# A rank search inside an attention loop: masks counted by VectorE instead of GpSimd and TensorE, and two context weights multiplied once

## What is computed

```
x = layernorm(x + attention0(x))        # 16 heads of width 8, plus a "splat" flow of 64 points
x = layernorm(x + cross0(x, context))   # the value path of the context: (c Wv^T + bv) Wo^T + bo
```

## Time and profile before

| | |
|---|---|
| median of 3 runs | 2092.27 us (2090.64 to 2105.77) |
| the profiled execution | 2103.81 us, span 2102.1 us |
| first loop, first to last score maximum | 46.13 to 493.35 us of the span |
| busy over the span: PE, PEld, DVE, ACT, POOL | 86%, 66%, 66%, 59%, 50% |
| granted TensorE clock, mean over the span | 0.90 of full |
| masks on GpSimd (line 946) | 128 x, 1563 ns each, 198.0 us busy |

### The profile page before, as it was taken

The page is one execution under the profiler, slowest core; times in us unless marked ns, Lnnn a source line. Parts: engine busy times, 40 slices in busy tenths (PEclk is TensorE's granted clock), DMA queues, the critical chain, the costliest instruction groups (busy, mean ns, idle before and its releaser), DMA issues. The chain is left out here.

```text
span 2102.1 us, 44035 instructions
## 1 busy us (share of the span) xinstructions
PE 1798.3 (86%) x15604; PEld 1391.5 (66%) x15604; DVE 1387.6 (66%) x4638; ACT 1247.6 (59%) x3006; POOL 1042.5 (50%) x1594
## 2 busy tenths in 40 slices
PE   3999999999588999999999999999849999569940
PEld 2666666666476778777777777877635666459940
DVE  3767777774467777777777887787646887341127
ACT  1465555654377777787777777776513777334412
POOL 0546655563335555565555565566421332246455
PEclk9789998996699999999999999999967999669975
DMA  4000000000200000000000000000000000054422
GB/s 56 9 6 14 14 15 14 8 11 8 85 1 1 5 1 7 7 7 7 7 4 4 7 7 7 4 5 5 7 24 9 22 27 19 17 117 79 66 59 81
DMA packets 70240, 44.81 MB, mean 21 GB/s; under 512 B 26560, under 2 KB 62538, under 8 KB 69834
## 3 DMA queue, kind: packets, MB, share of 16 engines
q1 hardware_dynamic: 55384, 29.79, 5.2%
q0 software_dynamic: 4608, 9.45, 3.1%
q10 hardware_dynamic: 10034, 2.77, 0.7%
HBM read 27.31 MB, written 14.16 MB: 20 GB/s over the span
## 5 line engine op out<-in xcount | busy, mean ns | idle before, releaser
L2105 POOL TENSOR_SCALAR probs<-probs,rsums 128x128 f32<-128x128 f32 (+1 forms) x512 | 208.3, 425 | 325.7 <-DVE rsums L2004 325.6
L946 POOL TENSOR_SCALAR at_least<-magnitudes,candidates 128x512 bf16<-128x512 f32 x128 | 198.0, 1563 | 210.6 <-DVE candidates L842 210.6
L1988 DVE CUSTOM_DVE_ANT_0 probs<-dist,pq,nmin 128x128 f32<-128x128 f32 (+1 forms) x512 | 181.2, 409 | 128.5 <-PE pq L1480 127.8
L1735 ACT ACTIVATE probs<-probs,low 128x130 f32<-128x130 f32 (+1 forms) x512 | 227.6, 460 | 3.7 <-DVE low L1988 3.6
L913 DVE TENSOR_REDUCE negmax<-ps_scores 128x4 f32<-128x1024 f32 x128 | 156.5, 1223 | 103.7 <-PE ps_scores L573 102.4
L731 ACT ACTIVATE pT<-ps_scoresT 128x1024 f32<-128x1024 f32 x128 | 131.2, 1025 | 77.4 <-PE ps_scoresT L582 70.4
L1998 DVE COPY pT<-pq 128x384 f32<-128x384 f32 x256 | 130.2, 550 | 2.7 <-PE pq L1495 2.7
L1657 ACT ACTIVATE qn<-pq 128x512 f32<-128x512 f32 x128 | 77.0, 602 | 79.9 <-PE pq L1352 78.4
L1480 PE MATMUL pq<-k1T,q1T 64*128 64x128 f32 (+1 forms) x1024 | 119.6, 352 | 1.5 <-DVE low L1988 1.4
L3083 POOL DMA_INDIRECT m_x<-token_rows,m_idx_put x80 | 75.8, 947 | 80.0 <-DVE m_idx_put L3013 32.8
L3035 DVE COPY m_y<-pm 128x256 f32<-128x256 f32 x40 | 17.0, 425 | 140.3 <-PE pm L2921 140.3
(11 more groups left out here) (527 smaller groups left out, 5545.4 us busy)
## 6 DMA issues: line engine op xcount, KB each, us to landing
expert_answers<-m_y SPq DMA_DIRECT2D x40, 128.0 KB, 2.1
m_w<-in_L_ffn_moe_w_dram SPq DMA_DIRECT2D x16, 256.0 KB, 6.0
x<-in_x_dram SPq DMA_DIRECT2D x16, 128.0 KB, 2.1
x_mid<-x SPq DMA_DIRECT2D x16, 128.0 KB, 1.8
y<-x_mid SPq DMA_DIRECT2D x16, 128.0 KB, 2.2
x_mid<-y SPq DMA_DIRECT2D x16, 128.0 KB, 1.8
cx<-x_mid SPq DMA_DIRECT2D x8, 256.0 KB, 3.1
token_rows<-c_hn SPq DMA_DIRECT2D x8, 256.0 KB, 2.0
```

What stands on the lines that cost most here:

```text
L946: pool.tensor_scalar(at_least[:, a, :], mags[:, 512 * (a // 2):512 * (a // 2) + 512], cf[:, a:a + 1], None, ALU.is_ge).then_inc(mask_ready ...
L1735: ins = act.activation(probs[:, a, keys_nulls(i, w)], probs[:, a, keys_nulls(i, w)], ACT.Exp, bias=low[:, a, i:i + 1], scale=-1.0, accum_o ...
L1988: ins = dve.tensor_tensor_reduce(probs[:, a + t, keys(i, w)], dist[:, (1 - t) * P:N], ps[:, t * P:t * P + w], slopes[h], nmin[u][:, t, h:h ...
L2105: ins = pool.tensor_scalar(probs[:, a + t, keys(i, w)], probs[:, a + t, keys(i, w)], rsums[:, a + t, i:i + 1], 1.0, ALU.mult, ALU.mult)
```

## The change

VectorE now makes the masks itself, with the form of compare that also adds up its result along the row (`row_counts`). A single product with ones sums the eight row counts over the partitions, and `decide` compares that product in PSUM with the ranks. Four mask instructions of a decision are spread over two steps; `decide` moves one step earlier. GpSimd keeps only its part of the normalisations in this loop.

For the context, Wv and Wo are multiplied once (`fold_cross`, at step 16 of the loop), with bv Wo^T added to the bias row; `three_parts` moves there. `cross_values` is gone, and `cross_out` multiplies the stored context `cT` (six buffers in place of two) with the folded weight.

```diff
@@ stages
-            (8, "max_rows"), (24, "mixed"), (27, "project_out"), (31, "cross_out"), (22, "normalise"),
-            (5, "decide0"), (9, "decide1"), (1, "candidates0"), (5, "candidates1"),
+            (8, "max_rows"), (24, "mixed"), (27, "project_out"), (16, "fold_cross"), (31, "cross_out"), (22, "normalise"),
+            (4, "decide0"), (8, "decide1"), (1, "masks00"), (2, "masks01"), (5, "masks10"), (6, "masks11"),
...
-            (-10, "project_x"), (-1, "vg"), (1, "cross_values"), (3, "influence_tm"), (6, "encode"),
-            (4, "count0"), (8, "count1"), (10, "transform"), (11, "read_transform"), (12, "decode"), (14, "flow"),
+            (-10, "project_x"), (-1, "vg"), (3, "influence_tm"), (6, "encode"),
+            (3, "count0"), (7, "count1"), (10, "transform"), (11, "read_transform"), (12, "decode"), (14, "flow"),
@@ TensorE
-            def cross_values(u):
-                pe.wait_ge(*cT_ready.at(u + 1))
-                ps = ring.open(pe, "vx", u, held=0.7)
-                pe.matmul(ps[:, 0:S_CTX + 1], wv_x[:], cT[u][:], start=True, stop=True).then_inc(ring.filled("vx", u), 1)
+            def fold_cross(u):
+                if u:
+                    return
+                pe.wait_ge(bias3_ready, 1)
+                ps = ring.open(pe, "w_x", held=0.9)
+                pe.matmul(ps[:, 0:D], wv_raw[:], wo_x[:], start=True, stop=True)
+                pe.matmul(ps[0:3, D:2 * D], bv_x[:], wo_x[:], start=True, stop=True).then_inc(ring.filled("w_x"), 1)
...
-                pe.wait_ge(*mask_ready.at(4 * (n + 1)))
                 pe.wait_ge(*small_ready.at(n + 1))
-                ps = ring.open(pe, "count", n, held=1.7)
-                for a in range(4):
-                    for q in range(8):
-                        pe.matmul(ps[:, a * 64:(a + 1) * 64], ones_bf[:], at_least[:, a, q * 64:(q + 1) * 64],
-                                  start=(q == 0), stop=(q == 7))
-                pe.matmul(ps[:, 256:272], ones_sq[:], at_least_small[:].rearrange("p a n -> p (a n)"),
-                          start=True, stop=True).then_inc(ring.filled("count", n), 1)
+                ps = ring.open(pe, "count", n, held=1.3)
+                pe.matmul(ps[:, 0:8], ones_sq[:], row_counts[:], start=True, stop=True).then_inc(ring.filled("count", n), 1)
...
-                    pe.matmul(ps[:, t * D:(t + 1) * D], vx[u][:, t * P:(t + 1) * P], wo_x[:], start=True, stop=False)
+                    pe.matmul(ps[:, t * D:(t + 1) * D], cT[u][:, t * S_CTX:t * S_CTX + P], w_x[:], start=True, stop=False)
@@ VectorE
-            three_parts(dve, setup, bo_x3, bo_x, bo_work, pick)
+            dve.tensor_copy(bv_x[:, 1:3], bv_x[:, 0:1].broadcast_to([P, 2])).then_inc(bias3_ready, 1)
...
+                link(dve.tensor_tensor(bo_x[:], bo_x[:], ps[0:3, D:2 * D], ALU.add))
+                dve.sem_inc(ring.read("w_x"), 1)
+                three_parts(dve, link, bo_x3, bo_x, bo_work, pick)
+                dve.sem_inc(parts_ready, 1)
...
+                for a in (2 * part, 2 * part + 1):
+                    chain.add(dve.tensor_scalar(at_least[:, a, :], mags[:, 512 * part:512 * part + 512], cf[:, a:a + 1], None,
+                                                ALU.is_ge, ALU.add, accum_out=row_counts[:, a:a + 1]))
+                if part:
+                    link(dve.tensor_tensor(at_least_small[:], mags_small[:], cf[:, 4:8].unsqueeze(2).broadcast_to([P, 4, 4]),
+                                           ALU.is_ge))
+                    dve.tensor_reduce(row_counts[:, 4:8], at_least_small[:], AX.X, ALU.add).then_inc(small_ready.sem, 1)
 
             def decide(n):
                 ps = ring.wait(dve, "count", n)
-                link(dve.tensor_reduce(counts[:, 0:4], ps[:, 0:256].rearrange("p (a n) -> p a n", a=4), AX.X, ALU.add))
-                dve.tensor_reduce(counts[:, 4:8], ps[:, 256:272].rearrange("p (a n) -> p a n", a=4), AX.X, ALU.add)\
-                    .then_inc(ring.read("count", n), 1)
+                dve.tensor_tensor(keep[:], ps[:, 0:8], need[:], ALU.is_ge).then_inc(ring.read("count", n), 1)
                 ring.wait_read(dve, "count", n)
-                link(dve.tensor_tensor(keep[:], counts[:], need[:], ALU.is_ge))
                 link(dve.copy_predicated(K["thr"][:], keep[:], cand[:]))
                 link(dve.tensor_scalar(bit[:], bit[:], 1, None, ALU.logical_shift_right))
@@ GpSimd
-            def masks(n):
...
-                for a in range(4):
-                    pool.tensor_scalar(at_least[:, a, :], mags[:, 512 * (a // 2):512 * (a // 2) + 512],
-                                       cf[:, a:a + 1], None, ALU.is_ge).then_inc(mask_ready.sem, 1)
```

More of the change, by code:

```diff
@@ L277, in loop_1 @@
         wo_raw = sb("xwo_raw", [P, D])
[L278 removed]
         wo_x = sb("xwo_T", [P, D])
[L280 removed]
+        w_x = sb("xw_folded", [P, D])
+        bv_x = sb("xbv", [P, 3])
         bo_x = sb("xbo", [3, D])
@@ L324, in loop_1 @@
         flowg = two("flowg", [P, 2, N])
-        cT = two("cT", [P, S_CTX + 1])
+        cT = sets(6, "cT", [P, S_CTX + P])
         csum = two("csum", [P, 1])
-        vx = sets(4, "vx", [P, N])
         oT = two("oT", [P, GROUPS, N])
@@ L628, in _ @@
                          q1=lambda u: project_qk(u, "q", wq, 1), k1=lambda u: project_qk(u, "k", wk, 1), vg=project_vg,
-                         distances=distances, cross_values=cross_values, influence_tm=influence_tm, gather=gather,
+                         distances=distances, fold_cross=fold_cross, influence_tm=influence_tm, gather=gather,
                          encode=encode, transform=transform, decode=decode, flow=flow,
@@ L656, in project_x, with fold_cross @@
                 act.wait_ge(*csum_ready.at(u + 1))
-                act.activation(cT[u][:, S_CTX:S_CTX + 1], csum[u][:], ACT.Copy, scale=1.0 / S_CTX)\
+                act.activation(cT[u][:, S_CTX:], csum[u][:].to_broadcast([P, P]), ACT.Copy, scale=1.0 / S_CTX)\
                     .then_inc(cT_ready.sem, 1)
-            def cross_values(u):
-                ps = ring.wait(act, "vx", u)
-                act.activation(vx[u][:, 0:S_CTX], ps[:, 0:S_CTX], ACT.Identity, bias=bv_x[:])
-                act.activation(vx[u][:, S_CTX:N], ps[:, S_CTX:S_CTX + 1].to_broadcast([P, N - S_CTX]), ACT.Identity,
-                               bias=bv_x[:]).then_inc(ring.read("vx", u), 1)
+            def fold_cross(u):
+                if u:
+                    return
+                ps = ring.wait(act, "w_x")
+                act.activation(w_x[:], ps[:, 0:D], ACT.Copy).then_inc(w_x_ready, 1)
             order = [("q", 0), ("k", 0), ("q", 1), ("k", 1)]
@@ L743, in _ @@
                          influence_tm=influence_tm, gather=gather, encode=encode, decode=decode, turn_rows=max_rows,
-                         cross_values=cross_values)
+                         fold_cross=fold_cross)
             with act.Fori(0, B // U) as it:
@@ L815, in split_qk, with fold_cross @@
                                          ALU.mult, ALU.add).then_inc(ring.read(name, u, half), 1)
+            def fold_cross(u):
+                if u:
+                    return
+                ps = ring.wait(dve, "w_x")
+                dve.wait_ge(w_x_ready, 1)
+                link(dve.tensor_tensor(bo_x[:], bo_x[:], ps[0:3, D:2 * D], ALU.add))
+                dve.sem_inc(ring.read("w_x"), 1)
+                three_parts(dve, link, bo_x3, bo_x, bo_work, pick)
+                dve.sem_inc(parts_ready, 1)
             def distances(u):
@@ L838, in transform, with candidates @@
                                   bt[:].rearrange("e (j h) -> e j h", h=2), ALU.add).then_inc(ring.read("trans", w), 1)
[L840 to L846 removed]
+            def candidates(n, part):
+                if part == 0:
+                    dve.wait_ge(dve_chain, chain.n)
+                    dve.tensor_scalar(cand[:], K["thr"][:], bit[:, 0:1], None, ALU.bitwise_or).then_inc(cand_ready.sem, 1)
+                    dve.wait_ge(*cand_ready.at(n + 1))
+                cf = cand[:].bitcast(F32)
+                for a in (2 * part, 2 * part + 1):
[5 more added lines that the diff above has]
+                    dve.tensor_reduce(row_counts[:, 4:8], at_least_small[:], AX.X, ALU.add).then_inc(small_ready.sem, 1)
             def decide(n):
                 ps = ring.wait(dve, "count", n)
[L850 to L852 removed]
+                dve.tensor_tensor(keep[:], ps[:, 0:8], need[:], ALU.is_ge).then_inc(ring.read("count", n), 1)
                 ring.wait_read(dve, "count", n)
[L854 removed]
                 link(dve.copy_predicated(K["thr"][:], keep[:], cand[:]))
@@ L917, in _ @@
                          split_q1=lambda u: split_qk(u, 2), split_k1=lambda u: split_qk(u, 3),
-                         candidates0=lambda u: candidates(2 * u),
-                         candidates1=lambda u: candidates(2 * u + 1), decide0=lambda u: decide(2 * u),
+                         masks00=lambda u: candidates(2 * u, 0),
```

(7 more changed lines are left out.)

26 lines of the change are left out of this document (10 added, 16 removed).

## The result

The changed kernel took **2153.7 us** (median of 4 runs, 2140.41 to 2163.49) beside 2093.99 of the kernel before (4 runs, 2090.64 to 2105.77): ratio **1.027, 95% interval 1.022 to 1.031** (the two medians alone give 1.029). The experiments ran on three chips, each with the kernel before beside it. They take longer for both kernels (before: 2142 us on each), so from here on ratios are compared, each to the kernel before on the same chip; 0.01 is 21 us. A repeat of the change gave 1.028 (1.025 to 1.032).

The account below looks back on a forecast made before the run. VectorE was taken to set most steps of the score loop, with one score buffer. Work +30 and clock +16 made +46 us: 2150 on the profiled execution's 2103.81, 2138 against the median, range 2100 to 2178.

Parts of the forecast that it names:

- Every step costs what the slower engine needs: Score loop: one score buffer keeps TensorE and VectorE within a step; VectorE sets six or seven of eight odd-item steps.
- Rival 1: Score loop: VectorE's added work falls into its idle time, TensorE's relief saves 33 us, giving 2059; chance 0.08.
- the price of a mask: A 512-column compare with sum on VectorE: 0.78 us from start to start, with 0.45 as the lower end.
- Rival 2: Masks on VectorE run at the plain rate, 0.33 us less each: 2097 to 2102 us; chance 0.15.
- The odd item: Item without `transform`, at full clock: VectorE's work per step sums to 27.7 us, against 24.28.
- hidden by little: Step 7: the count waits for step 6's masks, which end 0.75 us before the step does; no cost.
- The even item: Item with `transform`: steps sum to 33.0 us against 32.48, +0.5.
- the clock: TensorE idles more, so more low-clock stretches: 1 us an item, +16 us, ends 0 and +43.
- the 30 us of the other terms: Score loop: odd items +3.2 us on average, a pair of items +3.7, eight pairs +30 us.
- the forecast without more low clock: Lower end of the forecast's own range, given as 2115 us; the upper end is 2165.
- Rival 3: Score loop: VectorE's pace keeps TensorE idle and at half clock, +64 us on the +30, 2186; chance 0.10.
- The signs: Trace after: masks 0.7 us or more, VectorE's idle 102 to 40 or less, stretch 475 to 510, more stretches at 0.50.

Follow-up runs that it names:

- wide products: The 64 products of `transform` widened from 4 to up to 64 columns: ratio 0.988 on the kernel before, 1.008 on the change.
- filler: Constant products nobody reads: 24 ahead of step 6's transposes in the kernel before, 1.001; 32 ahead of q's product in the change, 1.026.

## Why the prediction was right, and where not

**Right: what bounds the loop.** "Every step costs what the slower engine needs" held. Steps 2 and 6 were to be 4.88 and 5.42 us and were 4.56 and 4.91, with no idle time before the next maximum; 1018 matmuls fewer bought nothing there. Half the mask columns gave their 2.1 us an item back in full. Rival 1 (TensorE's relief wins) is out.

**Close: the price of a mask.** I took 0.78 us between 0.45 and 0.78; it was 0.67. The rate of 1.05 ns a column was right, by the masks of two widths. The fixed part was not: the 0.51 us of the earlier trace rows is the distance to an instruction that uses the sum, and masks do not wait for each other's. Eight masks are 0.9 us an item less than I had. Rival 2 is out all the same, since 0.67 is far from its 0.45. The Trainium skill, VectorE: DVE Perf Modes, section "The perf-mode tier table", gives `tensor_scalar` of fp32 in SBUF twice the base rate. For the form that also sums this does not hold: it took 1.05 ns a column, and 743 ns for 512 columns against 426 ns for the plain form; here the measurement decides.

**The odd item: right sum, two errors in it.** 27.7 forecast, 27.66 found. VectorE's own work was 26.1, not 27.7. The rest is 0.78 us of idle time in each of steps 3 and 7, which I had at 2.40 and 2.50 without any. I had named the count's wait for its masks in step 7 as "hidden by little"; it is, with no idle time ahead of it. The error is in the price of the moved count: I took it as one small product, and left out its claim on a bank. It handed `values` a bank whose reader stands behind the maximum. That the sum came out at 27.7 all the same is luck: masks 0.9 us and other VectorE work 0.7 us too dear, two bank waits of 0.78 us left out.

**The even item: the clock too small.** I had +0.5 us plus 1 us an item for the clock. Full items are those behind the first two and ahead of the last. Even ones were 32.1 us on average before and 36.0 after, +3.9; odd ones 25.8 and 28.9, +3.0, where I had +3.2 plus the same 1 us. The 0.5 for the work itself was about right. With wide products, which keep TensorE at full clock in steps 2 to 5, steps 0 to 6 of an even item sum to 25.8 us in before and 26.0 in the change, and step 7 at full clock is 4.78 us in before and 5.12 in the change: together some 0.5 more. (The items themselves are 31.3 and 32.4 us; the difference of 1.1 has the low clock of step 7 in it.) So of the +3.9 some 3.4 us are clock: half-speed stretches that begin in or behind `transform`. In the change they last through steps 4 and 5 in three of seven full even items (six of seven in the repeat), at 9.13 us against 6.0 of my sum, and in three others they take step 7, 7.25 us. I placed the extra clock in odd items (step 7, at most 2.7 us). There it did not grow: about 1.5 us an item above full clock before, 1.2 after. It came in even ones.

**Sum.** +46 forecast; stretch +52.9 in the profiled execution, medians +60 (2153.7 against the 2138 forecast). The mis-sized term is the clock. I took 16 us; with the 30 us of the other terms taken off, it is about 23 us in this execution and 39 in the repeat (stretch 516.5), within my ends of 0 and 43. Two small slips in my sums changed nothing: 16 x 2.0 is 32, not 33 (rival 1), and the forecast without more low clock is 2092 + 30 = 2122, not 2115. Rival 3 (the low clock stays) came partly true and in another place: TensorE is busy without a gap at half clock for 22 us, and that stretch ends in the item.

**The signs.** Masks at 0.7 us or more: 0.75 long, 0.67 apart. Stretch 475 to 510: 500. More half clock: 0.79 against 0.88. Wrong: VectorE's idle time before its maximum was to fall from 102 to 40 us or less and is 87. It did leave six of eight steps of the odd item, but came back as the bank wait and in the low-clock steps of the even items.

## What to carry to other kernels

With one buffer between two engines, write each engine's work per step and take the larger; a product taken from TensorE is worth nothing in a step that VectorE sets, and work given to VectorE costs its full length there. When a stage moves in a kernel with a planned pool of buffers, follow the plan again: who gets which buffer, and where that buffer's last reader stands in its queue. And before feeding TensorE filler to hold its clock, look for thin products that can be widened in place: in this kernel that gave 1.2%, and filler gave nothing.

## What the runs showed of the hardware

- TensorE busy is not TensorE at speed: through `transform` it is busy without a gap in either form. With 4 columns a product the clock falls during it or behind it, to 0.50 (mean of step 3: 0.50 to 0.74). With up to 64 it was 0.97 to 1.00 in step 3 in all five kernels that have them. At full clock both forms take 3.90 us, so here the extra columns cost nothing.
- VectorE's compare that also sums along the row: 512 columns of fp32 743 ns, 256 columns 476 ns; pitch 0.67 and 0.40 us when the next instruction does not use the sum. The one example of 256 columns whose sum is used at once has 0.51.
- Filler moved the low clock rather than removing it. In before, 24 products kept step 7 of all full odd items at 1.00, made step 6 of even items 0.58 us longer, and step 2 of most even items took 6.4 us at 0.70, more than without filler; the runs came out even (1.001).
